# Second phase of a soft-MoE and recurrence kernel: all five engines' instructions in a new order

## Chip, cores and metric

The kernel runs on one core of one Trainium2 chip. The metric is the device time of one execution in microseconds. The core has five engines that run side by side, each with its own stream of instructions: TensorE (PE) for matmuls and transposes, ScalarE (ACT) for activation functions, VectorE (DVE), GpSimd (POOL), and SyncE (SP), which issues DMAs. They meet through semaphores.

## What is computed

Two layers over 16 sequences of 512 tokens of width 128. Each layer is `x = x + s * silu(ffn(xn))` with `xn = layernorm(x)`.

```python
# layer 0
Q = xn @ Wq + bq;  s = softmax(Q @ Q.T / sqrt(128)) @ Q
logits = xn @ phi.T + phi_b               # 8192 tokens x (64 experts * 32 slots)
D = softmax over slots;  C = softmax over experts
X = einsum('tznp,tzd->npd', D, xn);  X = tanh(layernorm(clip(X)))
Y = C @ (X @ expert_w + expert_b)         # then x = x + s * silu(Y)
# layer 1
a = exp(8 * sigmoid(x @ W_rg + b_rg) * log(sigmoid(lam)))
g = sqrt(1 - a*a) * sigmoid(x @ W_ig + b_ig) * (x @ W_in)
h[t] = a[t] * h[t-1] + g[t];  s = rmsnorm(h) @ W_out
r, k from x mixed with the token before;  ffn = sigmoid(r @ W_r) * (relu(k @ W_k)**2 @ W_v)
```

## The kernel before

The first phase (to about 600 us) makes the logits of all tokens, the exponentials `exp_slots` (stored to memory by tiles) and the expert inputs X, and a short middle part makes the expert outputs Y, kept as a high and a low part, `YHI` and `YLO`.

The second phase, which the change edits, goes through the 16 blocks of 512 tokens. One block is one sequence. For a block it does five things, spread over two or three passes of the loop, so that three blocks are in work at a time:

- **Combining experts**, 16 chunks `c` of 128 slots. SP loads exponentials (`exps`, L1178), POOL scales them two chunks at a time (`exps_weighed` to `weigh_exps`, L146), PE transposes a chunk into one of two banks `ct` (`exps_turned`, L1219), ACT copies it out rounded (`chunk_high`, tile `chi`, L1585), DVE takes the rest (`chunk_low`, `clo`, L1917), and PE adds three matmuls into `yac` (`combine`, L1229, L1230, L1232). `chi` and `clo` have three buffers.
- **Attention.** `project` (L1235 to L1237), `query` (ACT, L1534), `project_split` (DVE, L1924), `query_low` (POOL, L2275), `values` (PE, L1251), `value_high` (ACT, L1541), and for four row tiles `r`: `scores` (PE, L1265 to L1268), `row_max` (DVE, L1929), `probabilities` (ACT, an Exp, L1549), `weights` (DVE, L1938), `scaled` (ACT, L1569). Then for `k` of four: `turn` (PE, L1279), `turn_high` (ACT, `pth`, L1557), `turn_low` (DVE, `ptl`, L1948), `weigh` (PE, L1289 to L1292). `attended` (ACT, L1564) copies the result.
- **Joining layer 0.** `y_tanh` (ACT, L1577), `silu_y`, `gate_attended` (POOL, L2286), `residual`; then the layernorm: `mean` (PE, L1301), `squares` (ACT, L1590), `variance` (PE, L1309), `deviation_log` (ACT, a Ln, L1595), `deviation_inverse` (ACT, an Exp, L1600), `normalise` and its high and low parts.
- **Recurrence** of layer 1: `decay_gate`, `input_gate`, `input_product` on PE; on ACT `decay_tanh` (L1607), `decay` (Exp, L1612), `decay_squares` (L1619), `input_tanh` (L1640), `input_log` (Ln, L1670), `input_root` (Exp, L1675), after the scan on DVE `state_squares` (L1680), `state_log` (Ln, L1685), `state_inverse` (Exp, L1690).
- **Gate** of layer 1: `ffn_k`, `ffn_r`, `ffn_v` on PE, `ffn_k_relu`, `ffn_r_tanh` (L1647), `ffn_tanh` (Tanh, L1665) on ACT, and the output.

The order is written out by hand. Each engine's function (`sync2`, `tensor2`, `scalar2`, `vector2`, `gpsimd2`) defines small steps, each with its waits and one operation or a few, and below them lists the steps in the order in which that engine runs them: first a loop over `i` (L1770 for ACT) whose steps belong to blocks `i`, `i - 1`, `i - 2` and `i - 3`, then a written-out end for the last block, which works by halves of 256 tokens (`last_...`). An engine runs its list strictly in order, so a step that waits holds up all behind it.

ACT works with a table set that holds the functions it can evaluate. Two steps load one ahead of time: `log_table` (L1698, the set that has Ln and Exp) and `tanh_table` (L1702, the set that has Exp and Tanh). Copy, Identity, Square and Relu run with either. Where the program reaches a function that the set loaded last doesn't have, the build puts an `ACT_TABLE_LOAD` of its own in front of it, which then bears the line of that ACTIVATE; for a Ln it takes a set without Exp. Before, no ACTIVATE of the second phase has such a load.

```python
def log_table(i):
    if i >= 0:
        e.preload_act_table_set("natural_log_exp_and_others")
def tanh_table(i):
    if i >= 0:
        e.preload_act_table_set("exp_and_others")
```

## Time and profile before

| what | value |
|---|---|
| median of 3 runs | 1187.49 us (1187.18 to 1188.07) |
| profiled execution, span from first to last instruction | 1184.2 us, 3.3 below the median |
| busy in the span | PE 97%, DVE 89%, ACT 83%, POOL 81% |
| second phase | from about 602 us |
| one block of the second phase, from L1549 to L1549 | 35.0 us |
| loads of ACT's table sets in blocks 3 to 13 | 44, 1283 ns each |

The profile is one execution. Its page gives busy time of each engine, forty slices of the span with a digit for the busy tenths, the chain of waits that ended last, and groups of instructions with busy time, mean duration, and the idle time before them with what ended it. A line number is the line in the kernel. The trace behind it also answers by stretch of time, by engine and instruction by instruction.

### The profile page before, as it was taken

The page shows a single profiled execution, that of the slowest core. Times are in us where ns is not written, and L with a number is a line of the kernel's source. Part 1 is how long each engine was busy: PE and PEld are TensorE (multiplying, and loading weights), DVE is VectorE, ACT ScalarE, POOL GpSimd, SP SyncE. Part 2 cuts the span into 40 slices and gives each one's busy share as a digit, 9 for nine tenths or more (in the row PEclk, how much of TensorE's full clock was granted, in tenths as well). Part 3 has the DMA queues.
Part 4 walks back from the last instruction along what each step waited for, and adds up shares of the span by engine and source line. Part 5 has one row for each costly group of instructions (what it writes and reads, how often), then busy time and mean ns, then how long its engine had stood idle before and what let it go on. Part 6 is the DMA issues. An engine that isn't in the chain of part 4 may idle for free. (4 is left out here: it accounts for less than half of the span.)

```text
span 1184.2 us, 17639 instructions
## 1 busy us (share of the span) xinstructions
PE 1144.7 (97%) x5097; PEld 787.9 (67%) x5097; DVE 1050.1 (89%) x1608; ACT 981.7 (83%) x2128; POOL 958.9 (81%) x770
## 2 busy tenths in 40 slices
PE   5999999999999999999989999999999999999996
PEld 3666666565666666666457777777777777777764
DVE  7999999999999999999767888888888888888887
ACT  5877877877766766766668999999999999999998
POOL 3998999898999999999788777878777788877751
PEclk9999999999999999999999999999999999999999
DMA  4445435434424432443754444344444444444420
GB/s 131 152 152 200 141 140 182 153 128 164 155 109 160 155 133 113 161 156 129 225 188 154 131 142 143 119 147 128 142 143 143 131 128 134 141 128 142 142 72 18
DMA packets 125263, 167.36 MB, mean 141 GB/s; under 512 B 7536, under 2 KB 102000, under 8 KB 125040
## 3 DMA queue, kind: packets, MB, share of 16 engines
q1 hardware_dynamic: 123984, 165.71, 41.4%
q8 instruction: 42, 0.69, 0.2%
q10 hardware_dynamic: 1184, 0.53, 0.2%
q14 instruction: 53, 0.43, 0.1%
HBM read 90.71 MB, written 75.50 MB: 140 GB/s over the span
## 5 line engine op out<-in xcount | busy, mean ns | idle before, releaser
L146 POOL TENSOR_TENSOR exp_slots_loaded<-exp_slots_loaded,slot_max 128x1024 f32<-128x1024 f32 x128 | 323.2, 2545 | 6.6 <-DMA exp_slots_loaded<-exp_slots 3.2
L858 POOL TENSOR_TENSOR dd<-ed,rz 128x512 f32<-128x512 f32 x256 | 267.6, 1051 | 24.7 <-ACT rz L688 23.4
L563 PE MATMUL acc<-dd,xns 128*128 128x512 f32 x512 | 261.1, 592 | 0.7 <-POOL dd L858 0.7
L1917 DVE TENSOR_TENSOR clo<-ct,chi 128x512 fp32r<-128x512 f32 x256 | 171.5, 681 | 24.3 <-ACT chi L1585 21.6
L176 POOL TENSOR_TENSOR ch<-exp_slots_loaded 128x512 f32<-128x512 f32 x128 | 165.9, 1296 | 32.0 <-ACT exp_slots_loaded L666 30.9
L795 DVE TENSOR_REDUCE mr<-lg 128x16 fp32r<-128x512 f32 x256 | 168.0, 685 | 19.3 <-PE lg L506 16.9
L657 ACT ACTIVATE ed<-lg 128x512 f32<-128x512 f32 x256 | 145.6, 594 | 40.3 <-PE lg L540 38.4
L666 ACT ACTIVATE exp_slots_loaded<-lg 128x512 f32<-128x512 f32 x256 | 145.5, 594 | 26.4 <-PE lg L549 24.4
L1585 ACT ACTIVATE chi<-ct 128x512 fp32r<-128x512 f32 x256 | 147.7, 597 | 11.8 <-PE ct L1219 8.3
L1219 PE MATMUL ct<-identity,exp_slots_loaded 128*128 128x128 f32 x1024 | 150.9, 273 | 5.6 <-POOL exp_slots_loaded L146 3.1
L811 DVE TENSOR_REDUCE zd<-ed 128x32 f32<-128x1024 f32 x128 | 154.6, 1208 | 1.5 <-ACT ed L657 1.5
L804 DVE TENSOR_REDUCE mr<-lg 128x32 fp32r<-128x1024 f32 x128 | 155.5, 1215 | 0.0
L1219 PEld LDWEIGHTS ct<-identity,exp_slots_loaded 128*128 128x128 f32 x1024 | 124.0, 140 | 35.5 <-POOL exp_slots_loaded L146 8.4
L549 PE MATMUL lg<-shift_experts_to_slots,mt 128*128 128x512 f32 x256 | 144.9, 596 | 0.7 <-ACT ed L657 0.7
L504 PE MATMUL lg<-phi_then_expert_out,xn_transposed 128*128 128x512 f32 x256 | 140.7, 550 | 0.5 <-ACT exp_slots_loaded L666 0.3
L1229 PE MATMUL yac<-chi,phi_then_expert_out 128*128 128x512 f32 x256 | 128.5, 502 | 0.0
L563 PEld LDWEIGHTS acc<-dd,xns 128*128 128x128 f32 x512 | 95.6, 192 | 22.1 <-issue 2.9
L1232 PE MATMUL yac<-clo,phi_then_expert_out 128*128 128x512 f32 x256 | 102.4, 400 | 0.9 <-DVE clo L1917 0.9
L506 PE MATMUL lg<-phi_then_expert_out,xn_transposed 128*128 128x512 f32 x256 | 102.3, 399 | 0.0
L505 PE MATMUL lg<-phi_then_expert_out,xn_transposed 128*128 128x512 f32 x256 | 101.7, 397 | 0.0
L1230 PE MATMUL yac<-chi,phi_then_expert_out 128*128 128x512 f32 x256 | 101.5, 396 | 0.0
L549 PEld LDWEIGHTS lg<-shift_experts_to_slots,mt 128*128 128x128 f32 x256 | 48.2, 188 | 77.4 <-ACT ed L657 62.0
(315 smaller groups left out, 2500.2 us busy)
## 6 DMA issues: line engine op xcount, KB each, us to landing
exp_slots<-exp_slots_loaded SPq DMA_DIRECT2D x128, 512.0 KB, 3.4
exp_slots_loaded<-exp_slots SPq DMA_DIRECT2D x128, 512.0 KB, 3.5
xns<-xn_rows SPq DMA_DIRECT2D x128, 64.0 KB, 1.9
b_xraw<-in_xT SPq DMA_DIRECT2D x16, 256.0 KB, 3.8
out_t<-b_ti SPq DMA_DIRECT2D x15, 256.0 KB, 2.1
expert_w_late<-in_expert_w SPq DMA_DIRECT2D x5, 512.0 KB, 11.1
xn_rows<-slot_sum SPq DMA_DIRECT2D x8, 256.0 KB, 2.5
expert_w_early<-in_expert_w SPq DMA_DIRECT2D x3, 512.0 KB, 5.8
```

The source lines that it names most:

```text
L146: e.tensor_tensor(rows, rows, joined(SM, b)[:, h].unsqueeze(2).broadcast_to([P, TPB, GC * EPC, NP]), ALU.mult).then_inc(s_we)
L176: e.tensor_tensor(ch[v % 2][:, :], ec[v % RE][:, 0:BANK], ec[v % RE][:, BANK:HS], ALU.add).then_inc(s_ch)
L549: e.matmul(lg[v % 2][:, bank(k)], mt[v % 2][:, :], S2M[:, bank(k)], start=False, stop=True, skip_group_check=True).then_inc(s_s2)
L563: e.matmul(acc[k][:, :], xns[v % RX][:, :], dd[v % RX][:, bank(k)], start=tile == 0, stop=tile == NT - 1, skip_group_check=True).then_inc( ...
L657: e.activation(ed[v % RD][:, bank(k)], lg[v % 2][:, bank(k)], ACT.Exp).then_inc(s_ed)
L795: e.tensor_reduce(mr[v % 2][:, k * HN // 2:(k + 1) * HN // 2], lg[v % 2][:, bank(k)].rearrange("q (n p) -> q n p", p=NP), AX_X, ALU.max).t ...
L804: e.tensor_reduce(mr[v % 2][:, HN:G], lg[v % 2][:, :].rearrange("q (n p) -> q p n", p=NP), AX_X, ALU.max).then_inc(s_mx)
L811: e.tensor_reduce(zd[v % 2][:, :], ed[v % RD][:, :].rearrange("q (n p) -> q n p", p=NP), AX_X, ALU.add).then_inc(s_zd)
L858: e.tensor_tensor(dd[v % RX][:, bank(k)].rearrange("q (n p) -> q n p", p=NP), ed[v % RD][:, bank(k)].rearrange("q (n p) -> q n p", p=NP), ...
L1219: done = e.transpose(ct[c % 2][:, rows(k)], ECL[:, g // GC % RL, k, c % GC * P:(c % GC + 1) * P], IDENT[:, :])
L1585: e.activation(chi[g % RC][:, :], ct[c % 2][:, :], ACT.Copy).then_inc(c_h)
L1917: e.tensor_tensor(clo[g % RC][:, :], ct[c % 2][:, :], hi_f32(chi[g % RC][:, :]), ALU.subtract).then_inc(c_l)
```

## The change

Every list of steps of the second phase gets a new order: in the loop on all five engines, and in the written-out end on PE, ACT and DVE. No step is added or taken away, and no step's inside is changed. The core of the diff:

```diff
@@ sync2
                 for i in range(-2, NB + 3):
+                    load_x(i)
                     exps(i + 1, 2)
                     exps(i + 1, 4)
-                    load_x(i)
...
@@ tensor2
                     combine(i - 2, 11)
+                    exps_turned(i - 2, 13)
                     turn(i - 2, 1)
-                    exps_turned(i - 2, 13)
...
+                    input_gate(i - 3)
+                    combine(i - 1, 0)
+                    project(i - 1)
+                    input_product(i - 3)
                     exps_turned(i - 1, 2)
-                    input_gate(i - 3)
-                    input_product(i - 3)
-                    project(i - 1)
-                    combine(i - 1, 0)
                     exps_turned(i - 1, 3)
...
@@ scalar2
                     probabilities(i - 1, 1)
+                    log_table(i - 1)
+                    state_squares(i - 3)
                     chunk_high(i - 1, 6)
                     scaled(i - 1, 0)
-                    state_squares(i - 3)
-                    scaled(i - 1, 1)
                     probabilities(i - 1, 2)
                     chunk_high(i - 1, 7)
+                    ffn_tanh(i - 3)
+                    chunk_high(i - 1, 8)
+                    scaled(i - 1, 1)
+                    state_log(i - 3)
                     scaled(i - 1, 2)
-                    chunk_high(i - 1, 8)
-                    ffn_tanh(i - 3)
-                    log_table(i - 1)
-                    state_log(i - 3)
                     chunk_high(i - 1, 9)
+                    state_inverse(i - 3)
...
                     chunk_high(i - 1, 15)
+                    tanh_table(i - 1)
                     chunk_high(i, 0)
                     decay_tanh(i - 2)
+                    turn_high(i - 1, 3)
                     decay(i - 2)
-                    turn_high(i - 1, 3)
+                    y_tanh(i - 1)
                     decay_squares(i - 2)
                     chunk_high(i, 1)
-                    y_tanh(i - 1)
+                    attended(i - 1)
                     log_table(i - 1)
-                    attended(i - 1)
-                    input_log(i - 2)
-                    tanh_table(i - 1)
                     query(i)
+                    input_tanh(i - 2)
                     chunk_high(i, 2)
                     chunk_high(i, 3)
-                    input_tanh(i - 2)
+                    value_high(i)
+                    input_log(i - 2)
                     ffn_k_relu(i - 2)
-                    value_high(i)
                     input_root(i - 2)
...
                 last_state_log(1)
                 last_state_inverse(1)
+                log_table(LAST)
+                tanh_table(LAST)
...
@@ vector2
                     chunk_low(i - 1, 9)
+                    state_normalised(i - 3)
                     weights(i - 1, 3)
...
@@ gpsimd2
                 for i in range(-2, NB):
+                    if i < 0:
+                        exps_weighed(i + 1, 2)
+                    next_shifts(i + 2)
                     gate_attended(i)
                     query_low(i + 1)
-                    next_shifts(i + 2)
-                    if i < 0:
-                        exps_weighed(i + 1, 2)
```

The built program of the change has 183 `ACT_TABLE_LOAD` on ACT, that of before 69. Of one block in the loop it has 11, at L1595, L1702 (twice), L1698 (twice), L1640, L1670, L1675, L1665, L1685 and L1690; before there are 4, at L1698 (twice) and L1702 (twice). Two places of ACT's list show them. The first is ACT around `query` (L1534) in the middle of the loop, before:

```order
L1577 ACTIVATE b_ty<-yac 128x512
L1698 ACT_TABLE_LOAD
L1564 ACTIVATE b_st<-at 128x512
L1670 ACTIVATE b_a<-b_a,epsilons 128x512
L1702 ACT_TABLE_LOAD
L1534 ACTIVATE b_qf<-at,vectors 128x512
L1585 ACTIVATE chi<-ct 128x512 x2
L1640 ACTIVATE b_ti<-lp,derived_vectors 128x512
L1654 ACTIVATE b_kr<-lp 128x512
L1541 ACTIVATE r_vh<-at 128x512
L1675 ACTIVATE b_a<-b_a 128x512
```

and now:

```order
L1564 ACTIVATE b_st<-at 128x512
L1698 ACT_TABLE_LOAD
L1534 ACTIVATE b_qf<-at,vectors 128x512
L1640 ACT_TABLE_LOAD
L1640 ACTIVATE b_ti<-lp,derived_vectors 128x512
L1585 ACTIVATE chi<-ct 128x512 x2
L1541 ACTIVATE r_vh<-at 128x512
L1670 ACT_TABLE_LOAD
L1670 ACTIVATE b_a<-b_a,epsilons 128x512
L1654 ACTIVATE b_kr<-lp 128x512
L1675 ACT_TABLE_LOAD
L1675 ACTIVATE b_a<-b_a 128x512
```

`input_tanh` (L1640) moved ahead of the chunk copies and `input_log` (L1670) behind `value_high`; `tanh_table` (L1702) stood ahead of `query` and no longer does, and three loads stand at the ACTIVATEs' own lines.

The second is ACT from the third row tile's exponential (L1549) to `state_log` (L1685), before:

```order
L1569 ACTIVATE b_e<-b_e,epsilons,nmx 128x512
L1549 ACTIVATE b_e,nmx<-at,nmx 128x512
L1585 ACTIVATE chi<-ct 128x512
L1569 ACTIVATE b_e<-b_e,epsilons,nmx 128x512
L1585 ACTIVATE chi<-ct 128x512
L1665 ACTIVATE b_xr<-b_kr 128x512
L1698 ACT_TABLE_LOAD
L1685 ACTIVATE b_aa<-lp,epsilons 128x512
L1585 ACTIVATE chi<-ct 128x512
L1549 ACTIVATE b_e,nmx<-at,nmx 128x512
```

and now:

```order
L1549 ACTIVATE b_e,nmx<-at,nmx 128x512
L1585 ACTIVATE chi<-ct 128x512
L1665 ACT_TABLE_LOAD
L1665 ACTIVATE b_xr<-b_kr 128x512
L1585 ACTIVATE chi<-ct 128x512
L1569 ACTIVATE b_e<-b_e,epsilons,nmx 128x512
L1685 ACT_TABLE_LOAD
L1685 ACTIVATE b_aa<-lp,epsilons 128x512
L1569 ACTIVATE b_e<-b_e,epsilons,nmx 128x512
L1585 ACTIVATE chi<-ct 128x512
L1690 ACT_TABLE_LOAD
L1690 ACTIVATE b_aa<-b_aa 128x512
```

`log_table` (L1698) stood right ahead of `state_log` and is now further up; `ffn_tanh` (L1665), `state_log` and `state_inverse` (L1690) each have a load in front.

The third place is the start of the second phase on PE, before:

```order
L1219 MATMUL ct<-identity,exp_slots_loaded 128x128 x12
L1235 MATMUL at<-xn_transposed,weights_high 128x512
L1236 MATMUL at<-xn_transposed,weights_high 128x512
L1237 MATMUL at<-xn_transposed,weights_low 128x512
L1229 MATMUL yac<-chi,phi_then_expert_out 128x512
L1230 MATMUL yac<-chi,phi_then_expert_out 128x512
L1232 MATMUL yac<-clo,phi_then_expert_out 128x512
L1219 MATMUL ct<-identity,exp_slots_loaded 128x128 x4
```

and now:

```order
L1219 MATMUL ct<-identity,exp_slots_loaded 128x128 x8
L1229 MATMUL yac<-chi,phi_then_expert_out 128x512
L1230 MATMUL yac<-chi,phi_then_expert_out 128x512
L1232 MATMUL yac<-clo,phi_then_expert_out 128x512
L1235 MATMUL at<-xn_transposed,weights_high 128x512
L1236 MATMUL at<-xn_transposed,weights_high 128x512
L1237 MATMUL at<-xn_transposed,weights_low 128x512
L1219 MATMUL ct<-identity,exp_slots_loaded 128x128 x8
L1251 MATMUL at<-identity,b_qf 128x128 x4
```

`project` (L1235 to L1237) stood behind the transposes of three chunks and now stands behind those of two and the first `combine`.

The fourth is the same place on POOL, behind the branch into the phase, before:

```order
L146 TENSOR_TENSOR exp_slots_loaded<-exp_slots_loaded,slot_max 128x1024
L2275 TENSOR_TENSOR r_ql<-b_qf,r_qh 128x512
L146 TENSOR_TENSOR exp_slots_loaded<-exp_slots_loaded,slot_max 128x1024 x2
L128 TENSOR_TENSOR slot_sum<-slot_sum,slot_max 128x2x128
L130 TENSOR_TENSOR slot_joined<-slot_sum 128x128
L146 TENSOR_TENSOR exp_slots_loaded<-exp_slots_loaded,slot_max 128x1024 x3
```

and now:

```order
L146 TENSOR_TENSOR exp_slots_loaded<-exp_slots_loaded,slot_max 128x1024 x2
L2275 TENSOR_TENSOR r_ql<-b_qf,r_qh 128x512
L146 TENSOR_TENSOR exp_slots_loaded<-exp_slots_loaded,slot_max 128x1024
L128 TENSOR_TENSOR slot_sum<-slot_sum,slot_max 128x2x128
L130 TENSOR_TENSOR slot_joined<-slot_sum 128x128
L146 TENSOR_TENSOR exp_slots_loaded<-exp_slots_loaded,slot_max 128x1024 x4
```

One more scaling of exponentials (L146) now stands ahead of `query_low` (L2275).

## Rows read from the trace of the kernel before

**Rows 1.** The page: busy time and share of each engine; two engines in forty slices.

```profile
PE 1144.7 (97%) x5097; PEld 787.9 (67%) x5097; DVE 1050.1 (89%) x1608; ACT 981.7 (83%) x2128; POOL 958.9 (81%) x770
...
PE   5999999999999999999989999999999999999996
...
ACT  5877877877766766766668999999999999999998
```

**Rows 2.** Stretches: length, busy PE, PEld, DVE, ACT, POOL with counts, PEclk, DMA share, GB/s.

```profile
708.89:1093.61 384.72, 384.72 (x2004) 294.30 (x2003) 330.94 (x562) 375.25 (x651) 302.02 (x166) 1.00 0.43 136
641.43:673.91 32.48, 32.05 (x177) 25.43 (x177) 24.62 (x45) 31.41 (x55) 26.34 (x16) 1.00 0.44 138
1093.61:1128.44 34.83, 34.83 (x183) 26.68 (x182) 28.88 (x50) 33.94 (x60) 27.30 (x15) 1.00 0.44 136
1128.44:1184.20 55.76, 44.51 (x196) 29.92 (x194) 44.56 (x83) 47.26 (x86) 15.17 (x10) 0.96 0.12 38
```

**Rows 3.** Groups by line, blocks 3 to 13: busy us, mean ns, idle before.

```profile
L1948 DVE TENSOR_TENSOR ptl<-at,pth 128x512 fp32r<-128x512 f32 x44 | 30.0, 683 | 0.0
...
L1698 ACT ACT_TABLE_LOAD x22 | 28.2, 1283 | 0.4
L1702 ACT ACT_TABLE_LOAD x22 | 28.2, 1283 | 0.4
```

**Rows 4.** Timeline of ACT in one block: start us, length us, line, instruction.

```profile
872.13 0.82 ACT L1612 ACTIVATE b_aa<-b_aa,derived_vectors 128x512 f32<-128x512 f32 x1
872.86 0.57 ACT L1557 ACTIVATE pth<-at 128x512 fp32r<-128x512 f32 x1
873.33 0.62 ACT L1619 ACTIVATE b_a<-b_aa 128x512 f32<-128x512 f32 x1
873.86 0.58 ACT L1585 ACTIVATE chi<-ct 128x512 fp32r<-128x512 f32 x1
874.38 0.60 ACT L1577 ACTIVATE b_ty<-yac 128x512 f32<-128x512 f32 x1
875.00 1.28 ACT L1698 ACT_TABLE_LOAD   x1
876.29 0.60 ACT L1564 ACTIVATE b_st<-at 128x512 f32<-128x512 f32 x1
876.79 0.71 ACT L1670 ACTIVATE b_a<-b_a,epsilons 128x512 f32<-128x512 f32 x1
```

**Rows 5.** Waits in blocks 3 to 13: who, for whom, us in total, times, longest.

```profile
ACT b_f L1647 <- PE lp L1340: 2.1, 11, 0.2
```

**Rows 6.** Timeline at the start of the second phase, several engines.

```profile
593.85 0.74 POOL L120 TENSOR_TENSOR slot_max<-slot_max,slot_joined 128x256 f32<-128x256 f32 x1 [2.03 <-DVE slot_joined L116]
...
601.93 2.49 POOL L146 TENSOR_TENSOR exp_slots_loaded<-exp_slots_loaded,slot_max 128x1024 f32<-128x1024 f32 x1 [1.19 <-POOLq L1102]
...
604.88 0.47 PE L1235 MATMUL at<-xn_transposed,weights_high 128*128 128x512 f32 x1
605.20 0.39 PE L1236 MATMUL at<-xn_transposed,weights_high 128*128 128x512 f32 x1
605.43 0.40 PE L1237 MATMUL at<-xn_transposed,weights_low 128*128 128x512 f32 x1
...
607.09 1.28 POOL L2275 TENSOR_TENSOR r_ql<-b_qf,r_qh 128x512 fp32r<-128x512 f32 x1 [2.67 <-DVE r_qh L1924]
...
608.33 4.70 POOL L146 TENSOR_TENSOR exp_slots_loaded<-exp_slots_loaded,slot_max 128x1024 f32<-128x1024 f32 x2
...
610.73 0.66 PE L1219 MATMUL ct<-identity,exp_slots_loaded 128*128 128x128 f32 x4 [2.63 <-POOL exp_slots_loaded L146]
```

**Rows 7.** Busy time and PE's granted clock in two stretches with little matmul work.

```profile
600.00:610.00 10.00, 5.67 (x32) 3.90 (x30) 5.15 (x9) 3.52 (x7) 6.13 (x4) 1.00 0.48 151
1160.00:1175.00 15.00, 11.15 (x45) 6.42 (x43) 11.82 (x27) 14.88 (x30) 3.46 (x4) 1.00 0.00 0
```

**Rows 8.** Timeline at the end: the last ACTIVATE.

```profile
1180.03 0.42 ACT L1768 ACTIVATE b_e<-b_e 128x256 f32<-128x256 f32 x1
```

More of the change, by code:

```diff
@@ L1435, in tensor2 @@
                     exps_turned(i - 1, 0)
+                    weigh(i - 2, 1)
                     decay_gate(i - 3)
-                    weigh(i - 2, 1)
                     turn(i - 2, 3)
@@ L1465, in tensor2 @@
                     exps_turned(i - 1, 7)
-                    combine(i - 1, 6)
                     exps_turned(i - 1, 8)
                     state_mean(i - 3)
-                    scores(i - 1, 3)
+                    combine(i - 1, 6)
                     combine(i - 1, 7)
                     exps_turned(i - 1, 9)
+                    exps_turned(i - 1, 10)
+                    state_out(i - 3)
+                    mean(i - 2)
                     combine(i - 1, 8)
-                    exps_turned(i - 1, 10)
-                    mean(i - 2)
-                    state_out(i - 3)
                     combine(i - 1, 9)
@@ L1480, in tensor2 @@
                 turn(LAST, 0)
+                variance(LAST - 1)
                 exps_turned(LAST, 12)
-                variance(LAST - 1)
+                exps_turned(LAST, 13)
+                turn(LAST, 1)
+                weigh(LAST, 0)
                 combine(LAST, 10)
                 combine(LAST, 11)
-                turn(LAST, 1)
-                exps_turned(LAST, 13)
                 combine(LAST, 12)
                 exps_turned(LAST, 14)
-                weigh(LAST, 0)
                 turn(LAST, 2)
-                combine(LAST, 13)
-                exps_turned(LAST, 15)
                 decay_gate(LAST - 1)
                 weigh(LAST, 1)
+                exps_turned(LAST, 15)
                 turn(LAST, 3)
+                combine(LAST, 13)
                 combine(LAST, 14)
@@ L1848, in scalar2 @@
                 squares(LAST - 1)
[L1849 removed]
                 chunk_high(LAST, 11)
                 turn_high(LAST, 0)
+                deviation_log(LAST - 1)
                 chunk_high(LAST, 12)
[L1853 to L1854 removed]
                 deviation_inverse(LAST - 1)
                 turn_high(LAST, 1)
+                tanh_table(LAST)
+                scaled_k(LAST - 1)
                 chunk_high(LAST, 13)
                 chunk_high(LAST, 14)
[L1859 removed]
                 turn_high(LAST, 2)
                 scaled_r(LAST - 1)
+                decay_tanh(LAST - 1)
                 chunk_high(LAST, 15)
[L1863 removed]
                 decay(LAST - 1)
@@ L1867, in scalar2 @@
                 y_tanh(LAST)
+                input_log(LAST - 1)
                 log_table(LAST)
-                ffn_k_relu(LAST - 1)
+                input_root(LAST - 1)
                 last_squares(0)
-                input_log(LAST - 1)
+                tanh_table(LAST)
                 last_deviation_log(0)
```

183 lines of the change are left out of this document (88 added, 95 removed).

## Prediction

> **What bounds the kernel now.** I first read the busy row and the forty slices of the page [rows 1]. TensorE (PE) is busy 97% of the span. ScalarE (ACT) stands at 6 to 8 tenths through the first phase and at 9 from the 23rd slice on, in the second phase, which the change edits. So I cut the second phase into blocks, each from one block's first softmax exponential (L1549) to the next one's, and read busy time by stretch [rows 2]. Eleven whole blocks (708.89 to 1093.61) take 384.72 us, 34.97 each. PE is busy for all of it. ACT is busy 375.25, which is 34.11 a block, so ACT has only 0.86 us a block free. VectorE (30.1) and GpSimd (27.5) have 5 to 7 us. PE bounds the loop and ACT stands 2.5% behind it.
>
> Then I looked at what ACT does, for anything that the reordering changes in amount. In the eleven blocks there are 22 + 22 table loads of 1283 ns each [rows 3]: four a block, from the two `log_table` and two `tanh_table` calls. The timeline around one of them [rows 4] gives the full price. `y_tanh` (L1577) starts at 874.38 and runs 0.60 until the load at 875.00; `attended` (L1564) starts at 876.29. Where no load stands between, the next ACTIVATE starts before the last has ended: L1619 at 873.33, L1585 at 873.86, L1577 at 874.38; L1564 at 876.29, L1670 at 876.79. So a load costs its 1.28, 0.03 on its two sides, and the overlap that the ACTIVATE ahead loses (0.60 + 0.02 where 0.50 would do, 0.12): 1.42 to 1.43 us.
>
> **The change, part by part.** The source adds nothing, but the order of ACT's built program does. It has 69 table loads before and 183 after, 114 more. A load now stands at lines that never had one: L1640, L1670, L1675, L1665, L1685, L1690, L1595. The reason can be read off the rows of the change. `log_table` and `tanh_table` used to stand right ahead of the Ln and Tanh instructions; now they stand where the table they name isn't wanted next, and the build puts in a load of its own ahead of each function that the loaded set lacks. By L1549 to L1549 the counts are: block 0, 4 (as before); block 1, 7 (4); blocks 2 to 13, 11 each (4); block 14, 12 (4); block 15 to the end, 26 (7).
>
> Loop, blocks 2 to 13: ACT's work becomes 34.11 + 7 x 1.42 = 44.05 us. That is 9 us over PE's 34.97, so ACT sets the block. PE's own work doesn't change: the matmuls are the same. The other engines lie below 35 and gain cover. ACT's waits in the loop are three, each 0.2 us once a block, for PE (one row of the three stands there, L1647; L1585 and L1595 are like it) [rows 5], and PE now has slack. But new ones can come where ACT goes round through others. The tightest place I find is from `turn_high` 3 (L1557) to `attended`: VectorE's `turn_low` (0.68) [rows 3], the last `weigh` on PE (three matmuls that start 0.23 apart, as in [rows 6]) and the hand-overs, an estimate of about 1.7 us; ACT meanwhile has `decay` (0.73), `y_tanh` (0.50), `decay_squares` (0.53) and a `chunk_high` (0.50), 2.26 us by [rows 4]. If PE is late with combines 14 and 15 and the two weighs, that cover is just used up. I take 0.25 us of waits a block: 44.3. Bounds: none (44.05) and today's 0.86 (44.9). Blocks 2 to 13 add 12 x (44.3 - 34.97) = 112.0.
>
> Block 1: ACT busy 31.41 of 32.48 [rows 2]. 31.41 + 3 x 1.42 + 0.3 = 36.0, +3.5. Block 14: 33.94 + 8 x 1.42 + 0.3 = 45.6 against 34.83, +10.8.
>
> Block 15 and the written-out end, 55.76 us, ACT busy 47.26 [rows 2]. Of the 19 added loads two stand behind the last ACTIVATE (L1768) and cost nothing: after it (1180.03 + 0.42) ACT had nothing to do for 3.7 us, while VectorE and the store end the program [rows 8]. The other 17 at 1.40 (half-width ACTIVATEs lose less overlap) are 23.8 us, nearly all on the path, since ACT is busy 14.88 of the 15 us from 1160 to 1175 [rows 7]. ACT's waits inside the end were 55.76 - 47.26 - 3.7 = 4.8 us; longer stretches between its instructions cover some of them, and I keep 2.5. So 47.26 + 23.8 + 2.5 + 3.7 = 77.3, +21.5. Bounds: all 4.8 kept (+23.8), none kept (+19).
>
> Start of the phase: `combine` 0 now stands ahead of `project` on PE, and `project` ahead of the third chunk's transposes. Before, `project` stood behind these, which waited for GpSimd's first weighting (601.93 + 2.49), so L1235 came at 604.88 [rows 6]. Without that wait it can come about 1 us earlier. GpSimd's second weighting (2.35) now stands ahead of `query_low`, which was started at 607.09: it ends at about 606.8, shifts (0.74) follow, and `query_low` ends near 608.8 instead of 608.4. The fifth chunk's transposes and the scores, held until 610.73 by that weighting [rows 6], come about 2 us earlier. I take -2; bounds -3 and +1. The moves on SyncE (`load_x` ahead of two loads) and the other swaps on VectorE and PE touch engines with slack and cost nothing as long as ACT is the bound; without that cover they would be worth tenths of a microsecond a block.
>
> Sum on the profiled execution: -2 + 0 (block 0) + 3.5 + 112.0 + 10.8 + 21.5 = 145.8; 1184.2 + 145.8 = 1330.0. The median of the runs, 1187.49, lies 3.3 above that span, and I keep the 3.3: 1333.
>
> The Trainium skill ("ScalarE: Activation LUTs", section "What ACT_TABLE_LOAD costs") puts a drain of about 1380 ns behind each load's 1283 and calls a switch 2.66 us. The rows here show the load's length as stated and no drain: about 10 ns from load to next ACTIVATE [rows 4]. By the page's figure the estimate for the added loads would be nearly double the one above.
>
> **Rivals.**
> 1. Unneeded loads are free. One of the eleven in a block (the second L1702) asks for the set already loaded. No row of before shows such a load: all alternate. If it takes no time, 14 fewer count, 14 x 1.42 = 20 us: 1313. Against it: every load seen takes 1283 ns whatever stood before [rows 3].
> 2. New round trips. The old order was in step with PE, the new one has loads where it counted none; if ACT waits 2 us a block at places like `turn_high` 3 or between `deviation_log` and the mixes, that adds 14 x 1.8 = 25: 1358. For it: the cover at `turn_high` 3 is thin. Against it: PE has 9 us of slack a block.
> 3. Other side: faster. The added loads take no engine time, or are absorbed in ACT's gaps. The loop then stays PE's and only the start counts: 1187.5 - 2, and up to 4 from the end, 1184. It decides at 0.86 / 7 = 0.12 us a load. Against it: 44 of 44 loads at 1283 ns, with gaps of 0.02 around them [rows 3].
> 4. PE's clock. PE will be busy 79% of a block and idle in pieces. If its granted clock fell to 1.2 GHz, PE's 34.97 would become some 70 us a block: 12 x 35 more than now, about 1640. Against it: the clock stayed at 1.00 from 600 to 610 with PE busy 57% and from 1160 to 1175 with 74% [rows 7].
> 5. A load costs double, the price of [rows 4] no longer holding for loads that stand close together. Each of the 112 on the path (3 + 84 + 8 + 17) then takes another 1.42 us: about 1490. Nothing in the rows is for it; 44 loads of one length stand against it [rows 3]. The page's 2.66 us for a load would give nearly this time.
>
> **How the numbers follow.** Forecast 0.70; rival 1, 0.10; rival 2, 0.12; rival 3, 0.03; rival 4, 0.03; rival 5, 0.02. The forecast's own bounds: waits -3 to +8, end -2.5 to +2.3, start -1 to +3, load 1.31 (no overlap lost) instead of 1.42 -12: 1318 to 1345. To hold 8 in 10 the range reaches rivals 1 and 2: 1310 to 1356. About 0.2% (2.4 us) is what a measurement of this kernel can tell from no change. All cases but rival 3 are slower: slower 0.97, faster 0.02, same 0.01.
>
> **What would show it.** In the changed kernel's groups, table loads at L1640, L1670, L1675, L1665, L1685, L1690 and L1595, each 1283 ns. Blocks of about 44.3 us with ACT busy over 43.5 and PE idle some 9 of them, its waits ending on ACT. `ACT` at 9 tenths and `PE` at 7 in the later slices, PEclk at 9. In the chain of waits ACT in place of PE. The second L1702 of a block tells rival 1, the list of ACT's waits rival 2. I am wrong if blocks stay at 35 us, or if ACT is idle over 1.5 us in a block of 44 or more.

## The result and the profile after

The changed kernel takes 1334.68 us (median of 4 runs, 1334.09 to 1336.64) against 1187.51 for the kernel before in the same comparison (4 runs, 1187.18 to 1188.07): a ratio of 1.124, 95% interval 1.123 to 1.126. Its profiled execution has a span of 1332.3 us, 2.4 below its median; 148.1 us were added to the span of 1184.2.

The page of the kernel after, which answers to [rows 1]: busy times, then PE, ACT and PE's clock in forty slices, then the chain of waits by engine.

```profile
PE 1192.6 (90%) x5097; PEld 798.2 (60%) x5097; DVE 1080.2 (81%) x1608; ACT 1127.4 (85%) x2242; POOL 954.4 (72%) x770
...
PE   5999999999999999999989887888888889978874
...
ACT  5787787777676666667999999999999999999999
...
PEclk9999999999999999999989999999999989999997
...
ACT 32%; issue 11%; PE 7%; DVE 5%; ACTq 0%
```

ACT has 114 more instructions, all of them table loads (183 in all, 69 before), and takes PE's place in the chain of waits, where PE had 43% and ACT 2% in the kernel before. PE falls to 7 to 9 tenths in the second phase and ACT stands at 9 throughout.

Stretches of the kernel after from one block's first L1549 to the next one's, as in [rows 2] (length, busy PE, PEld, DVE, ACT, POOL, clock, DMA share, GB/s): block 0, block 1, blocks 2 to 13 together, block 14, block 15 and the end.

```profile
609.87:638.02 28.15, 27.87 (x161) 22.25 (x160) 21.46 (x39) 23.98 (x42) 24.13 (x15) 1.00 0.49 159
638.02:673.99 35.97, 34.51 (x186) 26.72 (x184) 25.57 (x46) 35.18 (x58) 26.64 (x17) 1.00 0.41 127
673.99:1211.11 537.12, 458.42 (x2184) 329.52 (x2184) 387.10 (x612) 517.07 (x794) 324.94 (x181) 0.97 0.34 106
1211.10:1256.96 45.86, 36.95 (x182) 26.55 (x182) 33.31 (x52) 44.15 (x67) 26.09 (x14) 1.00 0.35 112
1256.96:1332.30 75.34, 48.42 (x185) 31.55 (x185) 41.45 (x80) 72.01 (x105) 15.05 (x9) 0.83 0.07 22
```

A block of the loop takes 537.12 / 12 = 44.76 us, and ACT is busy 43.09 of it and idle 1.67. What grew, against [rows 2]:

| stretch | predicted | measured |
|---|---|---|
| start, to the first L1549 (613.03 before, 609.87 after) | -2 | -3.2 |
| block 0 | 0 | -0.2 |
| block 1 | +3.5 | +3.5 |
| blocks 2 to 13 | +112.0 | +117.4 |
| block 14 | +10.8 | +11.0 |
| block 15 and the end | +21.5 | +19.6 |
| sum | +145.8 | +148.1 |

Groups of table loads on ACT, and the scan on VectorE, in blocks 3 to 13 of the kernel after (busy us, mean ns, idle before), beside [rows 3]:

```profile
L1698 ACT ACT_TABLE_LOAD x22 | 28.2, 1283 | 0.4
L1702 ACT ACT_TABLE_LOAD x22 | 28.2, 1283 | 0.4
L1665 ACT ACT_TABLE_LOAD x11 | 14.1, 1283 | 0.2
...
L1675 ACT ACT_TABLE_LOAD x11 | 14.1, 1283 | 0.2
...
L2020 DVE TENSOR_TENSOR_SCAN b_hh<-b_aa,vectors,b_ti 128x512 f32<-128x512 f32 x11 | 38.5, 3503 | 0.0
```

L1685, L1690, L1595, L1640 and L1670 read as L1665 does: 22 + 22 + 7 x 11 = 121 loads, 11 a block. All take 1283 ns, also the second L1702 of a block, which asks for the set that is loaded. The last row holds what I had not looked at: the recurrence's scan takes 3.50 us, where it took 1.37 in the same blocks of the kernel before. ACT's only wait of any size from 700 to 1090 us is for it:

```profile
ACT b_a L1680 <- DVE b_hh L2020: 12.2, 9, 1.4
```

So I had two things to explain: what the loads cost by themselves, and what the rest of the new order costs, which the loads cover.

### The profile page after: what moved, and what is told of

Read it like the earlier page. It is cut to its first block, busy times and chain, and to the rows that moved or that the text cites. A ratio compares the mean times of both kernels' runs of the same rounds, so it can differ in the third digit from the quotient of the medians.

```text
span 1332.3 us, 17753 instructions
## 1 busy us (share of the span) xinstructions
PE 1192.6 (90%) x5097; PEld 798.2 (60%) x5097; DVE 1080.2 (81%) x1608; ACT 1127.4 (85%) x2242; POOL 954.4 (72%) x770
## 4 chain that ended last, share of the span: by engine, by line
ACT 32%; issue 11%; PE 7%; DVE 5%; ACTq 0%
ACT chi L1585 5%; DVE b_hh L2020 3%; ACT b_e L1569 3%; ACT L1698 2%; ACT L1702 2%; ACT b_e L1549 1%; ACT L1665 1%; ACT L1670 1%; ACT L1685 1%; ACT L1690 1%; PE ct L1219 1%; PE at L1279 1%; ACT pth L1557 1%; PE yac L1229 1%; PE yac L1232 1%
## 5 line engine op out<-in xcount | busy, mean ns | idle before, releaser
L146 POOL TENSOR_TENSOR exp_slots_loaded<-exp_slots_loaded,slot_max 128x1024 f32<-128x1024 f32 x128 | 316.0, 2485 | 39.0 <-DMA exp_slots_loaded<-exp_slots 24.4
L1219 PE MATMUL ct<-identity,exp_slots_loaded 128*128 128x128 f32 x1024 | 149.5, 278 | 19.0 <-DVE clo L1917 18.2
L804 DVE TENSOR_REDUCE mr<-lg 128x32 fp32r<-128x1024 f32 x128 | 155.5, 1215 | 0.0
L1585 ACT ACTIVATE chi<-ct 128x512 fp32r<-128x512 f32 x256 | 148.6, 596 | 5.2 <-PE ct L1219 5.0
L1219 PEld LDWEIGHTS ct<-identity,exp_slots_loaded 128*128 128x128 f32 x1024 | 122.2, 143 | 46.3 <-issue 29.4
L1229 PE MATMUL yac<-chi,phi_then_expert_out 128*128 128x512 f32 x256 | 148.4, 580 | 1.0 <-ACT chi L1585 0.6
L2280 POOL TENSOR_TENSOR r_xl<-xn,r_xh 128x512 fp32r<-128x512 f32 x15 | 19.2, 1280 | 136.4 <-DVE r_xh L1974 136.4
L1232 PE MATMUL yac<-clo,phi_then_expert_out 128*128 128x512 f32 x256 | 106.1, 415 | 10.7 <-DVE clo L1917 10.6
L1230 PE MATMUL yac<-chi,phi_then_expert_out 128*128 128x512 f32 x256 | 103.7, 405 | 0.0
```

Source lines behind the costliest of these rows:

```text
L146: e.tensor_tensor(rows, rows, joined(SM, b)[:, h].unsqueeze(2).broadcast_to([P, TPB, GC * EPC, NP]), ALU.mult).then_inc(s_we)
L804: e.tensor_reduce(mr[v % 2][:, HN:G], lg[v % 2][:, :].rearrange("q (n p) -> q p n", p=NP), AX_X, ALU.max).then_inc(s_mx)
L1219: done = e.transpose(ct[c % 2][:, rows(k)], ECL[:, g // GC % RL, k, c % GC * P:(c % GC + 1) * P], IDENT[:, :])
L1229: e.matmul(yac[:, :], YHI[:, c, :], chi[g % RC][:, :], start=c == 0, stop=False)
L1585: e.activation(chi[g % RC][:, :], ct[c % 2][:, :], ACT.Copy).then_inc(c_h)
```

## Experiments: loads and order apart

Each experiment names the kernel that it starts from; a block's length and busy times are those of its one profiled execution. "Block" is again from L1549 to L1549, in the loop's steady part.

**placed_oldend and placed_loop.** The kernel after, with the two table steps put back in ScalarE's loop right ahead of the functions that need them, so that the build adds none of its own. `placed_loop` has all other lists of the kernel after; `placed_oldend` has the written-out ends of TensorE, ScalarE and VectorE from the kernel before as well.

```diff
@@ scalar2, loop
+                    tanh_table(i - 1)
                     ffn_r_tanh(i - 3)
...
-                    log_table(i - 1)
...
+                    log_table(i - 1)
                     state_log(i - 3)
...
-                    tanh_table(i - 1)
                     deviation_inverse(i - 2)
...
+                    chunk_high(i, 0)
                     tanh_table(i - 1)
-                    chunk_high(i, 0)
                     decay_tanh(i - 2)
...
-                    log_table(i - 1)
                     query(i)
...
+                    log_table(i - 1)
                     input_log(i - 2)
```

Expected of `placed_oldend`: 

> The changed kernel, with log_table and tanh_table in the loop each moved right ahead of the first instruction that needs its set (state_log, decay_tanh, input_log, ffn_r_tanh), so that a block has 4 loads again instead of 11, and with the written-out ends of PE, ACT and DVE as they were before the change. Everything else in the new order. Theory (the added loads are the whole loss): blocks fall from 44.75 to 34.97 us, PE is the bound again, and the start keeps the 3.2 us that it gained (first L1549 at 609.87 instead of 613.03): 1187.5 - 3.2 = 1184.3, between 1183 and 1186. Rival (the new order of the other engines costs by itself, hidden now under ACT): blocks above 35.3 us, 1193 or more. A second rival: the gain at the start is given back by the first blocks, 1187.5.

Expected of `placed_loop`: 

> As placed_oldend, but with the changed kernel's own written-out ends, which keep their added loads: the build has 89 rows of loads on ACT instead of 183 (69 before the change), 20 more than before, of which 2 stand behind the last ACTIVATE. Theory: 18 loads that count at about 1.2 to 1.4 us give 22 to 25 us over placed_oldend: 1206 to 1210. Rival: the new order of the ends is worth something that the loads hide; then the difference is under 18 us.

Measured: `placed_oldend` 1219.05 us, ratio 1.028 (1.026 to 1.029); `placed_loop` 1240.50, ratio 1.045 (1.044 to 1.047). Taking the added loads out of the loop, together with the new written-out ends, returns 115.6 of the 147 us. The new written-out end costs 21.4: near the 21.5 of the prediction, and just under the 22 to 25 expected here. But 31.5 us stay, and the rival was right: with four loads a block the blocks take 37.4 to 37.9 us, not 35.0. Waits of ACT in `placed_oldend` from 700 to 1090 us (total, times, longest), and two of its blocks:

```profile
ACT b_qf L1534 <- PE at L1237: 14.7, 11, 1.4
ACT b_a L1680 <- DVE b_hh L2020: 12.4, 10, 1.2
ACT pth L1557 <- PE at L1279: 9.0, 10, 1.2
```

```profile
786.20:823.92 37.72, 36.06 (x184) 26.66 (x183) 32.16 (x51) 33.85 (x60) 26.67 (x16) 1.00 0.39 126
823.92:861.30 37.38, 35.74 (x184) 26.74 (x183) 31.73 (x51) 33.85 (x60) 26.74 (x16) 1.00 0.40 128
```

No engine is busy throughout here: PE is busy 35.7 of 37.4 and ACT 33.9. ACT waits for the projection, for the scan and for a transpose, 3.5 us a block.

**no_second_tanh and squares_back.** Two ways to take something off ACT in the kernel after: the unneeded second tanh load goes (10 loads a block), or `state_squares`, which waits for the scan, goes two steps back to where it stood.

```diff
@@ no_second_tanh
                     chunk_high(i - 1, 15)
-                    tanh_table(i - 1)
...
@@ squares_back
-                    state_squares(i - 3)
                     chunk_high(i - 1, 6)
                     scaled(i - 1, 0)
+                    state_squares(i - 3)
```

Expected of `no_second_tanh`: 

> The changed kernel without the second of its two tanh_table calls in the loop (the one behind chunk_high 15), which asks for the set that is loaded already: 15 loads fewer, 10 in a block. Theory (a load of the set that is there costs what any load costs): 14 blocks of 1.3 to 1.4 us less, 1334.7 - 19 = 1316. Rival (such a load is free or cheap): 1334.

Expected of `squares_back`: 

> The changed kernel with state_squares (L1680) on ACT moved back behind chunk_high 6 and scaled 0, where it stood before the change; all loads stay. In the changed kernel ACT waits 1.36 us a block there for the scan on DVE (L2020). Theory (the wait is a slot filled too early and nothing else hangs on it): 14 x 1.36 = 19 us less, 1316. Rival (DVE's chain then is late elsewhere, since the load ahead of it moves with the work): under 5 us less, 1330 or more.

Measured: 1333.66 (ratio 1.124, 1.122 to 1.125) and 1333.98 (1.124, 1.123 to 1.126). Neither gives anything, and neither of my explanations held. The load isn't free: it takes its 1283 ns in the kernel after, and where it is gone ACT is idle 2.83 us a block instead of 1.67, and the block takes 44.7 as before. Waits of ACT in `no_second_tanh`:

```profile
ACT b_a L1680 <- DVE b_hh L2019: 12.2, 9, 1.4
ACT b_aa L1607 <- PE lp L1237: 6.6, 9, 0.7
ACT b_ty L1577 <- PE yac L1232: 3.6, 9, 0.4
```

(One line less in the file makes L2020 L2019.) The wait for the scan is as long as it was, and two waits for PE have come up at the place of the load. In `squares_back` the wait for the scan is gone from the list and others stand in its place, 0.8 a block for a transpose (L1585 for L1219) and 0.2 for a maximum. So the block is not ACT's work plus a wait. The chain of waits of `no_second_tanh` in one block (start, length, engine, line) goes round through several engines:

```profile
854.51 3.48 DVE b_hh L2019
...
876.42 0.64 ACT b_ty L1600
877.08 0.69 DVE xn L1966
...
887.59 0.24 PE at L1237
888.56 0.46 ACT L1640
```

From the scan to L1600 it runs mostly on ACT; from there VectorE's `normalise` and `turn_low` and then 9.4 us of PE without a pause lead to `input_tanh` (L1640), beside the place where the load was taken out. Both variants and the kernel after have the 3.5 us of the scan in common, so I looked there next. (The load taken out and the scan made short together were not run.)

**Why the scan takes 3.5 us.** The timeline of the kernel before around the scan (start, length, engine, line), VectorE and GpSimd:

```profile
850.04 0.69 DVE L2012 SCALAR_TENSOR_TENSOR b_ti<-b_ti,b_a 128x512 f32<-128x512 f32 x1
850.16 0.89 POOL L130 TENSOR_TENSOR slot_joined<-slot_sum 128x128 f32<-128x128 f32 x1
...
850.76 1.37 DVE L2020 TENSOR_TENSOR_SCAN b_hh<-b_aa,vectors,b_ti 128x512 f32<-128x512 f32 x1
...
851.01 3.32 POOL L146 TENSOR_TENSOR exp_slots_loaded<-exp_slots_loaded,slot_max 128x1024 f32<-128x1024 f32 x1
```

And the kernel after:

```profile
853.77 0.76 DVE L2012 SCALAR_TENSOR_TENSOR b_ti<-b_ti,b_a 128x512 f32<-128x512 f32 x1
...
854.57 3.51 DVE L2020 TENSOR_TENSOR_SCAN b_hh<-b_aa,vectors,b_ti 128x512 f32<-128x512 f32 x1
...
854.61 2.38 POOL L146 TENSOR_TENSOR exp_slots_loaded<-exp_slots_loaded,slot_max 128x1024 f32<-128x1024 f32 x1 [0.63 <-DVE b_ti L2012]
```

Before, GpSimd was still joining sums (L130) when the scan began; its weighting (L146) came 0.25 us later and took 3.32 instead of some 2.4. After, GpSimd is ahead of its work and stands at the wait that `exps_weighed(i, 4)` has for the scan's input (L2012). The same semaphore lets it go 0.04 us behind the scan's start, and now the scan is the one that is long: it ends 1.1 us behind the weighting. In both cases the two run as if one after the other. The kernel before shows the second case too, once: in block 15, where GpSimd also stands at that wait, the scan starts at 1130.58 and takes 3.52, the weighting at 1130.62 and takes 2.40. The Trainium skill ("GPSIMD Engine Reference", section "1. Specifications") has GpSimd's SBUF interfaces shared with VectorE, with contention where a VectorE instruction has two SBUF inputs. The scan and the weighting both read two, and the rows agree that they hold each other up; who goes first and for how long the other is held is read here from the rows.

**after_scan_first and po_scan_first.** GpSimd waits for the reciprocal that VectorE runs between the scan's input and the scan. Neither wait guards data that the weighting touches; both only time it.

```diff
@@ exps_weighed
                         if k == 4 and i >= 2:
-                            e.wait_ge(S["gt"], i - 1)
+                            e.wait_ge(A["z"], i * TPB + 1)
```

Expected of `after_scan_first`: 

> The kernel after, with one wait of GpSimd changed: its weighting 4 of a block waits for VectorE's first reciprocal behind the scan's input (weights 0, L1938) instead of for the scan's input (L2012). In the kernel after the scan (L2020) starts at 854.57 and that weighting (L146) at 854.61, 0.04 apart; the scan takes 3.51 us and ends 1.1 behind the weighting. In the kernel before the scan (850.76) had 0.25 us on the weighting (851.01), took 1.37, and the weighting took 3.32 instead of 2.38: the two seem to take turns, and who is first goes on. Theory: with the 0.15 us that the reciprocal takes the scan comes first and takes 1.4 us, the weighting behind it 3.3; ScalarE's wait for the scan at L1680 (1.36 a block) goes, blocks go from 44.75 to about 43.4 to 43.8, and the time to 1316 to 1321. Rival A (the scan is slow whenever GpSimd's weighting runs, whoever is first): scan stays at 3.5, time 1334. Rival B (the scan becomes short, but another wait takes the place of this one, as in the two experiments that took work off ScalarE): scan 1.4, time over 1330.

Expected of `po_scan_first` (the same edit to `placed_oldend`): 

> The same change of GpSimd's wait, made to the version with four loads a block (placed_oldend, 1219.05, blocks of 37.4, where ScalarE waits 1.2 a block for the scan at L1680, 1.4 for the projection at L1534, 0.9 for the transposes of weights at L1557). Theory: scan 1.4, the wait at L1680 goes, blocks of 36.2, 1219 - 14 x 1.2 = 1202. Rival A: scan 3.5, 1219. Rival B: scan 1.4, but the other two waits grow by as much, over 1215.

Measured: `after_scan_first` 1328.33 (ratio 1.119, 1.117 to 1.120), `po_scan_first` 1212.30 (1.021, 1.020 to 1.022). In both the scan takes 1.28 us, in every block. The timeline of `after_scan_first`:

```profile
852.06 1.28 DVE L2020 TENSOR_TENSOR_SCAN b_hh<-b_aa,vectors,b_ti 128x512 f32<-128x512 f32 x1
...
852.17 3.36 POOL L146 TENSOR_TENSOR exp_slots_loaded<-exp_slots_loaded,slot_max 128x1024 f32<-128x1024 f32 x1 [0.70 <-DVE nmx L1938]
```

Whether the weighting starts 0.04 or 0.11 us behind the scan decides which of the two is 1 to 2 us longer. Rival A falls. ACT's wait at L1680 is gone from both lists. The gain, 6.4 us, lies between the theory (1316 to 1321) and rival B (over 1330), and the clock column says why. Three neighbouring blocks of `after_scan_first`:

```profile
805.91:850.52 44.61, 39.81 (x182) 28.86 (x182) 30.29 (x51) 43.21 (x67) 27.17 (x16) 0.92 0.33 107
850.52:893.88 43.36, 36.90 (x182) 26.57 (x182) 30.14 (x51) 43.03 (x67) 27.11 (x16) 1.00 0.35 110
893.88:938.42 44.54, 38.24 (x182) 27.86 (x182) 30.34 (x51) 43.14 (x68) 27.17 (x16) 0.96 0.34 108
```

Where PE's granted clock held, the block is 43.36 with ACT idle 0.33: the full 1.4 us is gained. Only 3 of blocks 2 to 13 are so. The other 9 take 44.53 to 44.61, and in all of them the clock's mean is 0.92 or 0.96. In the third block above there is a short fall from 2.4 to 1.2 GHz:

```profile
895.80:899.00 3.20, 3.20 (x11) 2.63 (x10) 2.54 (x6) 3.17 (x6) 3.20 (x2) 0.50 0.00 0
```

PE had been busy 3.14 of the 5.00 us ahead of the fall (890.7 to 895.7), and 3.14 of the 5.00 us ahead of the same place in the block before, in which the clock held. Behind the fall, at 901.17, ACT waits 1.08 for PE's transposes (L1585). Each of the nine long blocks has this wait, of 1.07 to 1.09, and the three short ones have none. So a new wait takes most of the gain, and it goes with the falls of the clock, not with the order alone. In `po_scan_first` most blocks fall from 37.4 to 36.85, and the time, 1212.30, lies between the theory (1202) and rival B (over 1215): from 700 to 1090 us the waits for the projection (14.7 in all) and the turn (8.9) are as they were, and those for a transpose rise from 0.6 to 8.3 in all.

**Does the clock matter in the kernel after itself?** Two of its blocks:

```profile
718.74:763.50 44.76, 40.00 (x182) 28.80 (x182) 32.15 (x51) 43.10 (x67) 27.04 (x16) 0.92 0.34 105
897.79:942.55 44.76, 36.99 (x182) 26.54 (x182) 32.20 (x51) 43.08 (x68) 27.07 (x16) 1.00 0.34 105
```

No. PE is busy 3 us longer in the first and the block is as long. The clock falls at nearly the same place as above (0.50 from 720.1 to 723.3), but ACT waits there for the slow scan, until 723.79, and finds the transposes done when it goes on. So in these blocks the wait for the scan covers the fall.

## Experiments: which list the order's cost comes from

**po_old_pe, bf_new_act, act_alone.** `po_old_pe` is `placed_oldend` with TensorE's loop in the old order. `bf_new_act` is the kernel before with ScalarE's loop from `placed_oldend` (new order, four loads). `act_alone` is the kernel before with ScalarE's whole list from the kernel after (183 loads). Each of the three has 2 runs.

Expected of `po_old_pe`: 

> The version with four loads a block (placed_oldend, 1219.05) with TensorE's loop in the order of the kernel before; the loop lists of ScalarE, VectorE, GpSimd and SyncE stay new. Theory: the waits of ScalarE at L1534 and L1557 (2.3 a block) come from TensorE's new order (input_gate and combine 0 ahead of project, exps_turned 13 and 14 ahead of the turns), so blocks fall from 37.4 by 1.5 to 2.3 to about 35.1 to 35.9, and the time to 1187 to 1198. Rival: they come from what TensorE itself waits for in ScalarE's and VectorE's new order, and blocks stay above 37: over 1213.

Expected of `bf_new_act`: 

> The kernel before with ScalarE's loop in the new order with the four loads put back ahead of the functions that need them (as in placed_oldend, 1219.05); all other lists old, four loads a block. Theory (the new order costs through ScalarE's own list): blocks 36.5 or more, over 1209. Rival (it costs through the lists of TensorE, VectorE and GpSimd): blocks 35 to 35.5, 1187.5 to 1195.

Expected of `act_alone`: 

> The kernel before with ScalarE's list of the kernel after alone, loop and end: 183 loads, 11 a block; the other four engines keep the old order. Theory (the new lists fit one another; ScalarE's alone leaves the others out of step, as TensorE's old list did in the experiment before): the waits in a block are longer than in the kernel after, blocks over 45, 1337 to 1370. Rival (the waits that four loads a block laid bare come from the new order of the other engines): blocks of 44.1 to 44.4, about 1187.5 + 139 + 0 = 1322 to 1330.

| kernel | ACT's order | others' order | loads a block | time, us (ratio) | block, us | ACT idle, us |
|---|---|---|---|---|---|---|
| before | old | old | 4 | 1187.5 | 34.97 | 0.86 |
| `placed_oldend` | new | new | 4 | 1219.1 (1.028) | 37.4 to 37.9 | 3.5 to 4.1 |
| `po_old_pe` | new | new, PE old | 4 | 1253.7 (1.056; 1.054 to 1.058) | 39.2 to 40.2 | 5.0 to 5.9 |
| `bf_new_act` | new | old | 4 | 1257.8 (1.059; 1.056 to 1.062) | 40.0 | 6.0 |
| after | new | new | 11 | 1334.7 (1.124) | 44.76 | 1.67 |
| `act_alone` | new | old | 11 | 1357.4 (1.143; 1.140 to 1.146) | 46.0 | 2.8 |

My theory for `po_old_pe` was wrong, by 55 us or more: the waits for the projection and the turn don't come from TensorE's new order. With the old one they are there too (1.8 and 0.75 a block), ACT waits 0.9 for the values besides, and PE waits 2.0 for `chunk_low`. `bf_new_act` settles it. ScalarE's new list against four old ones costs 5 us a block; the new lists of the other engines win back some 2.5 of these. Its waits of ACT:

```profile
ACT b_a L1680 <- DVE b_hh L2020: 19.7, 10, 2.0
ACT b_qf L1534 <- PE at L1237: 16.5, 10, 1.7
ACT r_vh L1541 <- PE at L1251: 14.0, 10, 1.4
```

So the source of the order's cost is ScalarE's list, and the four other lists fit it better than the old ones do. `act_alone` says the same with the loads in place: 22.7 us more than the kernel after. Which of ScalarE's moved steps it is was not taken apart. The costs of loads and order don't simply add. The added loads, with ScalarE's written-out end, cost 99.5 us where the other lists are old (`act_alone` less `bf_new_act`) and 115.6 where they are new (after less `placed_oldend`): ACT's idle time falls by 3.2 us a block in the first case and by 1.9 in the second, so the loads cover waits that the order makes.

**before_plus7.** The reverse: all orders old, loads added. One more table step ahead of each of the seven functions, asking for the set that is loaded anyway.

```diff
@@ scalar2, loop of the kernel before
+                    tanh_table(i - 3)
                     ffn_tanh(i - 3)
                     log_table(i - 1)
+                    log_table(i - 3)
                     state_log(i - 3)
...
+                    tanh_table(i - 2)
                     input_root(i - 2)
```

Expected: 

> The kernel before with 7 more table loads in each pass of ScalarE's loop, one ahead of ffn_tanh, state_log, state_inverse, deviation_log, input_log, input_tanh and input_root, each asking for the set that is loaded already; every order stays old. 95 loads more: 4 in block 1, 7 in blocks 2 to 14. Theory (loads are ScalarE's time, and the rest of the kernel after's loss is the order): ScalarE's 34.11 a block becomes 44.05, blocks 44.05 to 44.9, 1187.5 + 4.6 + 13 x (9.1 to 9.9) = 1310 to 1321. Rival A (a load of the set already there is cheaper than the others): blocks under 43, under 1297. Rival B (loads stretch round trips through VectorE and TensorE beyond their own time, whatever the order): blocks over 45.5, over 1328.

Measured: 1322.76, ratio 1.114 (1.111 to 1.116). There are 82 more loads, not 95: of two that stand one right behind the other for the same set (at `state_log`) the build keeps one, so a block has 10. One block and ACT's largest wait:

```profile
813.72:858.45 44.73, 37.73 (x182) 26.16 (x182) 33.13 (x52) 42.36 (x66) 26.63 (x15) 1.00 0.34 107
```

```profile
ACT b_a L1680 <- DVE b_hh L2027: 17.7, 9, 2.0
```

With 10 loads and the old order the block is as long as with 11 and the new one. (One of its 13 blocks takes 46.3, with the clock at 0.96.) The number lies between the theory and rival B: 135 us for 82 loads, 1.65 each, more than a load takes. The surplus has a name again: the scan (L2027 in this file) takes 3.51 us. It takes 3.5 in every kernel here that keeps GpSimd's wait and has longer blocks than the kernel before (`placed_oldend`, `po_old_pe`, `bf_new_act`, `act_alone`, this one): GpSimd is then ahead of its work and goes with the semaphore, whatever the order.

**plus7_scan_first2.** `before_plus7` with GpSimd's other wait, as in `after_scan_first`.

Expected: 

> The kernel before_plus7 (old orders, 10 loads a block, 1322.76, blocks of 44.73, ScalarE idle 2.37 a block, of it 2.0 in the wait for the scan at L1680, scan 3.51) with GpSimd's fourth weighting waiting for VectorE's weights 0 instead of for the scan's input. Theory: the scan comes first again and takes 1.3 to 1.4, the wait of 2.0 goes, and in the old order nothing takes its place: blocks of 42.7 to 43.0, 1322.8 - 14 x 1.9 = 1296 to 1300. Rival (as in the kernel after with the same change, another wait takes over most of it, whatever the order): scan short, blocks over 44, over 1314.

Measured: 1291.11, ratio 1.088 (1.086 to 1.090), 31.7 us less, and 5 better than the theory's range. The scan takes 1.28. Two neighbouring blocks:

```profile
678.39:720.88 42.49, 36.98 (x182) 26.27 (x182) 30.30 (x52) 42.12 (x66) 27.05 (x15) 1.00 0.35 112
720.88:765.00 44.12, 38.61 (x182) 27.68 (x182) 29.08 (x52) 42.50 (x66) 27.04 (x15) 0.96 0.34 108
```

Ten of the thirteen whole blocks from block 2 on take 42.2 to 42.5 with ACT idle 0.37; three take 44.12, all with the clock at 0.96. In the blocks at full clock ACT is the bound, and a load's price is plain: (42.49 - 34.97) / 6 = 1.25. It is less than its own 1.28 because ACT's old idle time fell from 0.86 to 0.37, while its work other than loads rose by 0.31. Over the whole kernel it is 103.6 us / 82 = 1.26, but this takes in the three slow blocks (1.6 us each) and a gain at the end: the last block's scan is short too, and block 15 takes 53.5 instead of 55.8. The same wait in the kernel before might so be worth some 2 us, an estimate; it was not run.

**start_both.** The first L1549 came 3.2 us earlier in the kernel after. Only that part is taken over: TensorE's and GpSimd's new loop order for the first three passes, the kernel before otherwise.

```diff
@@ tensor2, and gpsimd2 in the same way
                 for i in range(-2, NB):
+                    if i < 1:
+                        ...
+                    else:
...
```

Expected: 

> The kernel before, with TensorE's and GpSimd's new loop order in the first three passes of the loop (i below 1) and the old order from there on; all other lists are as before. Theory: the first softmax exponential of the phase comes 2 to 3.2 us earlier, as in the kernel after (609.87 against 613.03), and all behind it with it: 1184.3 to 1185.5. Rival: the gain at the start is given back in block 0 or 1, where TensorE or GpSimd have no slack, or the first exponential came early through another engine's order: 1187.3 within 0.6.

Measured: 1184.30, ratio 0.997 (0.996 to 0.998), as the theory had it. It is the one version here that beats both kernels, by 0.3%. Its first exponential is at 611.06, 2.0 earlier than before, and block 1 gives another 0.6; the blocks behind are 35.0 as ever. Its span is 2.1 us shorter, its median 3.2. About 1 us of the first exponential's place varies from one execution to the next: with the same order at the start it comes at 610.12 in `placed_oldend` and at 611.38 in `po_scan_first`.

## Why the prediction was right

The time came out at 1334.7 against 1333, on the mechanism that had 0.70: ScalarE's table loads. The terms, by the prediction's own steps:

- **The count and length of the loads held**: 183, eleven a block, 1283 ns each. Rival 1 falls, since the unneeded load takes its full time; that its removal gains nothing is the ring's doing. Rivals 3 and 5 fall with the same rows. The Trainium skill's drain of about 1380 ns ("ScalarE: Activation LUTs", section "What ACT_TABLE_LOAD costs") doesn't show: in the kernel after a load that changes the set ends at 1328.32 and its ACTIVATE starts at 1328.34 (rows below).
- **The price of a load, 1.42, was too high.** ACT's busy time rose by 43.09 - 34.11 = 8.98 a block, 1.283 for each of the seven loads. The work that isn't loading is 28.98 in both kernels, so of the 0.12 of lost overlap that I read from one place [rows 4] nothing is left in this sum. That is 0.96 us a block too much, and ACT was busy 43.09, not the over 43.5 that I had named as a sign. A part of it is the new order: `placed_oldend`, with four loads, is busy 33.85 instead of 34.11, and against it the seven loads add 9.24, 1.32 each. In the old order the six added loads are 1.38 each in `before_plus7` (42.36 - 34.11) and 1.34 in `plus7_scan_first2` (42.12).
- **The waits, 0.25, were too low.** ACT is idle 1.67. Of it 1.36 is the wait for the scan, at L1680, not at `attended`, where I had found the tightest place; no wait stands there. That is 1.4 too little. By the prediction's own test (idle over 1.5 in a block of 44 or more) this step is wrong. The two errors cancel in part: 44.3 forecast, 44.76 measured, +5.4 over twelve blocks; the start and the end, 3.1 less than forecast together, take up more of it. So the sum was right to 2 us, and partly by luck. Rival 2 named new round trips at other places and another size.
- **The other swaps were to cost nothing "as long as ACT is the bound".** For the other engines' own time that held, but ACT isn't the bound in the sense meant: one experiment took a load of 1.28 us off it, another the wait for the scan, and neither gained anything. And "tenths of a microsecond a block" without that cover was wrong: `placed_oldend` shows 2.4, and `bf_new_act` 5 for ScalarE's list alone. I had costed the moves by the engines' free time, which says nothing of who waits for whom.
- **Block 1 and block 14** came out at +3.5 and +11.0 (+3.5, +10.8).
- **The end**: ACT's busy time rose by 72.01 - 47.26 = 24.75, of which 2.57 are two loads behind the last ACTIVATE, as said. The other 17 are 22.2, 1.30 each, where I took 23.8. The waits inside are 2.4 (2.5), the tail 3.5 (3.7). Sum +19.6 for +21.5. `placed_loop` against `placed_oldend` gives 21.4 for the written-out end.

The last ACTIVATE with the load ahead of it and the two behind it, beside [rows 8]:

```profile
1327.04 1.28 ACT L1768 ACT_TABLE_LOAD   x1
1328.34 0.42 ACT L1768 ACTIVATE b_e<-b_e 128x256 f32<-128x256 f32 x1
1328.77 1.28 ACT L1698 ACT_TABLE_LOAD   x1
...
1330.06 1.28 ACT L1702 ACT_TABLE_LOAD   x1
```

- **The start** gained 3.2, just past my bound of 3. The mechanism was the one named: `project` at 603.96 instead of 604.88, and GpSimd's second weighting ahead of `query_low`. That starts at 606.85 all the same (607.09 before) and ends at 608.1, where I had expected 608.8. Beside [rows 6]:

```profile
603.96 0.39 PE L1235 MATMUL at<-xn_transposed,weights_high 128*128 128x512 f32 x1
...
606.85 1.28 POOL L2275 TENSOR_TENSOR r_ql<-b_qf,r_qh 128x512 fp32r<-128x512 f32 x1 [0.36 <-DVE r_qh L1924]
...
608.09 2.40 POOL L146 TENSOR_TENSOR exp_slots_loaded<-exp_slots_loaded,slot_max 128x1024 f32<-128x1024 f32 x1
...
609.87 0.69 ACT L1549 ACTIVATE b_e<-at,nmx 128x512 f32<-128x512 f32 x1 [1.09 <-DVE nmx L1933]
```

- **Rival 4**: PE's clock did not stay at 1.2 GHz, but it no longer held at 1.00 either (0.97 over blocks 2 to 13), and PE was idle 6.6 us a block, not 9. The falls cost nothing in these blocks and 1.2 us in each of nine blocks of `after_scan_first`. In block 15 and the end the clock is 0.83; what that costs is not shown.
- **The forecast's own bounds** were added up a little too narrow: the parts named give 1314 to 1346, not 1318 to 1345. Nothing else hangs on it.

## What to carry to other kernels

Read a new order of ScalarE's list first for where each function finds its table: here, taken out of the kernel after, the added loads are worth 115.6 us, and 31.5 stay. A block's length with one engine 96% busy can still be set by a ring of waits through others; the test is to take a known 1.3 us off that engine, and here it returned nothing. And where VectorE and GpSimd are let go by one semaphore, look at both their durations: here less than 0.1 us decided which of them was held.

## What the runs showed of the hardware

- A VectorE scan (128x512, two inputs) and a GpSimd multiply (128x1024, two inputs) that start together run as one after the other: 1.28 to 1.37 and 3.3 us if the scan leads by 0.11 to 0.25 us, 3.5 and 2.4 if it leads by 0.04.
- A table load of the set that is already loaded takes 1283 ns like any other (the second L1702 of each block, and the 82 of `before_plus7`).
- PE's granted clock falls to 1.2 GHz for short stretches in some blocks of kernels whose PE is busy in pieces (in `after_scan_first` 36.9 of 43.4 us in a block at full clock), and holds at 2.4 in the kernel before, where PE has no pause (1.00 over 384.72 us, [rows 2]). In `plus7_scan_first2` a block with the clock at 0.96 is 1.63 us longer (44.12 against 42.49). Why it falls in some blocks and not in others of the same kernel stays open.
